# Four exponentials of a batch's token attention in one group instead of two pairs

## The reference

```
qkv = x @ W_qkv + b_qkv                      # per batch of 512 tokens
attn = (q @ k^T) * SCALE                     # 512 x 512
attn = attn * mult(sigmoid(attn))            # mult steps through 0.1, 0.3, 1, 1.5, 2
attn = softmax(attn)
out = (attn @ v) @ W_proj + b_proj
```

## Time and profile before

| | us |
|---|---|
| median of three runs | 492.12 |
| the profiled execution | 494.61 |
| its span, first to last instruction | 492.8 |
| PE busy | 476.9 |
| DVE busy | 315.8 |
| POOL busy | 310.8 |
| ACT busy | 263.2 |
| PE's granted clock, share of full | 0.996 |

### The profile page before, as it was taken

The page is one execution under the profiler, slowest core; times in us unless marked ns, Lnnn a source line. Parts: engine busy times, 40 slices in busy tenths (PEclk is TensorE's granted clock), DMA queues, the critical chain, the costliest instruction groups (busy, mean ns, idle before and its releaser), DMA issues.

```text
span 492.8 us, 6482 instructions
## 1 busy us (share of the span) xinstructions
PE 476.9 (97%) x2037; PEld 341.8 (69%) x2037; DVE 315.8 (64%) x724; ACT 263.2 (53%) x478; POOL 310.8 (63%) x314
## 2 busy tenths in 40 slices
PE   8898999998999998999999998999999999999997
PEld 7776766676676665676676766677666777778886
DVE  3747453655697758388855883569866565867563
ACT  3395636546725592338752659324773456355551
POOL 5364797429859383485563565467676585678773
PEclk9998999999999999999999999999999999999999
DMA  7700000000000000000000000000000000000000
GB/s 246 237 0 2 0 1 1 0 1 1 1 1 1 1 0 1 1 1 1 0 1 1 0 1 1 1 0 1 23 0 1 1 22 1 0 1 6 18 0 22
DMA packets 7934, 7.37 MB, mean 15 GB/s; under 512 B 732, under 2 KB 7772, under 8 KB 7900
## 3 DMA queue, kind: packets, MB, share of 16 engines
q1 hardware_dynamic: 7900, 6.96, 4.4%
HBM read 5.91 MB, written 1.05 MB: 14 GB/s over the span
## 4 chain that ended last, share of the span: by engine, by line
PE 78%; ACT 4%; DVE 3%; issue 2%; POOL 1%; DVEq 0%; ACTq 0%; POOLq 0%
PE bank L1308 19%; PE bank L1123 16%; PE bank L1125 16%; PE bank L1124 16%; PE bank L1346 3%; PE bank L1244 1%; PE bank L1146 1%; ACT L768 1%; DVE pr L1012 1%; PE bank L1338 1%; ACT xnB L665 1%; PE bank L1358 1%; PE bank L1316 1%; PE bank L1252 1%; PE bank L1286 1%
## 5 line engine op out<-in xcount | busy, mean ns | idle before, releaser
L645 POOL TENSOR_TENSOR t<-t,sl 128x512 f32<-128x512 f32 x105 | 147.7, 1413 | 84.5 <-DVE t L1064 65.2
L768 ACT ACTIVATE sl<-bank 128x512 f32<-128x512 f32 x168 | 99.2, 596 | 129.7 <-PE bank L1125 112.8
L1308 PE MATMUL bank<-t,WD 128*128 128x512 f32 x260 | 128.8, 592 | 0.0
L1064 DVE TENSOR_TENSOR t<-bank,sbc 128x512 f32<-128x512 f32 x105 | 72.3, 688 | 66.1 <-PE bank L1125 63.2
L1123 PE MATMUL bank<-xhF,WGh 128*128 128x512 f32 x167 | 90.6, 543 | 0.0
L645 POOL TENSOR_TENSOR t<-t,sbc 128x512 f32<-128x512 f32 x63 | 80.9, 1313 | 1.1 <-DVE t L1064 0.9
L1064 DVE TENSOR_TENSOR t<-bank,sl 128x512 f32<-128x512 f32 x63 | 43.2, 687 | 58.8 <-ACT sl L768 29.2
L1123 PE MATMUL bank<-xhF,WUh 128*128 128x512 f32 x168 | 67.0, 399 | 2.3 <-DVE t L1064 2.3
L1125 PE MATMUL bank<-xhF,WUl 128*128 128x512 f32 x168 | 66.7, 397 | 0.0
L1124 PE MATMUL bank<-xlF,WUh 128*128 128x512 f32 x168 | 66.5, 396 | 0.0
L1125 PE MATMUL bank<-xhF,WGl 128*128 128x512 f32 x167 | 66.4, 398 | 0.0
(11 more groups left out here) (209 smaller groups left out, 723.8 us busy)
## 6 DMA issues: line engine op xcount, KB each, us to landing
stage<-in_gate SPq DMA_DIRECT2D x7, 192.0 KB, 6.1
stage<-in_up SPq DMA_DIRECT2D x7, 192.0 KB, 6.3
WD<-in_down SPq DMA_DIRECT2D x7, 192.0 KB, 6.2
X<-in_x SPq DMA_DIRECT2D x4, 256.0 KB, 5.4
out<-X SPq DMA_DIRECT2D x3, 256.0 KB, 2.3
raw<-in_small SPq DMA_DIRECT2D x1, 384.0 KB, 4.3
out<-X SPq DMA_DIRECT2D x2, 128.0 KB, 2.1
raw<-in_small SPq DMA_DIRECT2D x1, 192.0 KB, 2.7
```

What stands on the lines that cost most here:

```text
L645: pool.tensor_tensor(t2[k % NT2][:, :], t2[k % NT2][:, :], by[:, :], ALU.mult).then_inc(a_done, 1)
L768: act.activation(sl[k % NSL][:, :], bank[k % 2][:, :], ACT.Silu).then_inc(silu_done, 1)
L1064: dve.tensor_tensor(t2[k % NT2][:, :], bank[2 + k % 2][:, :], by[:, :], ALU.mult).then_inc(t2_done, 1)
L1308: r = pe.matmul(OACC[:, :], WD[:, c, :], t2[k % NT2][:, :], start=(c == 0), stop=(c == CH - 1 or k == TAIL[0] - 1))
```

## The change

The two steps `bexp` 0 and `bexp` 1 are taken from offset 17 of each batch's thread and put at offset 23, ahead of `bexp` 2 and `bexp` 3. Nothing else is changed in the text.

```diff
--- before.py
+++ after.py
@@ -95,9 +95,9 @@
 ROUTED_LATE = (0, 1, 2)
 B_STEPS = [(0, "stats"), (1, "rstd"), (2, "xn"), (4, "xT"), (5, "xl"), (7, "bqk", 0), (8, "bqkl", 0), (11, "bs", 0), (11, "bsp", 0, 0), (12, "bsp", 0, 1), (12, "bsp", 0, 2), (13, "bsp", 0, 3),
            (14, "bs", 1), (14, "bsp", 1, 0), (15, "bsp", 1, 1), (15, "bsp", 1, 2), (16, "bsp", 1, 3),
-           (17, "bexp", 0), (17, "bexp", 1), (17, "bs", 2), (17, "bsp", 2, 0), (18, "bsp", 2, 1),
+           (17, "bs", 2), (17, "bsp", 2, 0), (18, "bsp", 2, 1),
            (18, "bsp", 2, 2), (19, "bsp", 2, 3), (20, "bs", 3), (20, "bsp", 3, 0),
-           (21, "bsp", 3, 1), (21, "bsp", 3, 2), (22, "bsp", 3, 3), (23, "bexp", 2), (23, "bexp", 3),
+           (21, "bsp", 3, 1), (21, "bsp", 3, 2), (22, "bsp", 3, 3), (23, "bexp", 0), (23, "bexp", 1), (23, "bexp", 2), (23, "bexp", 3),
            (25, "bpT", 0), (26, "bpT", 1), (26, "bpT", 2), (27, "bpT", 3),
            (28, "bo", 0), (29, "bo", 1), (30, "bw"), (30, "byx")]
 F_STEPS = [(0, "stats"), (1, "rstd"), (2, "xn"), (4, "xT"), (5, "xl"), (6, "route"), (7, "inner", 0), (8, "rt"), (9, "rexp"),
```

## The result

The changed kernel took 496.15 us (median of 20 runs, 494.09 to 498.05) against 493.37 us (20 runs, 490.76 to 495.64): ratio 1.0065, 95% interval [1.0047, 1.0083]. It is slower by 3.2 us, 2.3 to 4.1. The forecast was +1.37 us, within 1%: right in sign and in staying within 1%, but less than half of the size. Two single executions, 801.44 us of the kernel before and 965.86 us of a variant, were of a much slower state and are left out of every comparison.

What follows compares the result with a forecast made beforehand. PE, busy 97%, bounds the kernel, so ACT's relief counts only where PE waited. Terms -0.75 + 0 + 0 + 1.44 + 0.68 = +1.37 us on 492.12 give 493.5 us; range 489.3 to 497.1.

Steps and rivals of the forecast that it cites:

- Where the steps go: Planner's order: only ACT's queue changes; two exponentials per batch move from slots 49, 69, 86, 108 to 55, 75, 92, 114.
- Removed: Early block off ACT: eight table loads, 10.26 us; PE gains 0.75 us in batch 0, nothing in batches 1 to 3.
- Added, batch 0: Late Silu 56 ends 1.44 us later; PE stands 0.39 before gate 58, absorbed by L1012 behind POOL's run: 0 us.
- Rival A: Batch 0's early block was dearer, all three DVE waits go: -0.67 us, 491.5, or -2.79, 489.3; chance 0.17.
- rival B: POOL's bunched products lock DVE out in batches 1 to 3: +7.5 us, 499.6; chance 0.06.
- Batch 1: Late Silu becomes 249.46, gate product starts 249.95, 0.49 us to spare: 0 us, at most +0.95.
- Batch 2: Late block delays the copy PT by the full 1.44; PE's 1.39 wait becomes 2.83 less 0.57: +1.44 us.
- Batch 3: Late Silu ends at 366.37, gate product started at 365.69: +0.68 us, between 0 and 1.44.
- The base: Profiled execution 494.61 us, PE clock near full, so the +1.37 is carried over to the runs' median of 492.12.
- C: Every late block costs its full 1.44 us: +5.0 us, 497.1; chance 0.07.
- D: ACT's relief counts in full: -10.3 us, 481.9 (-2.1%); chance 0.03.
- E: The change does not do what it says, planner shifts other steps or loads stay: within +-1 us; chance 0.07.

Runs made afterwards that it cites:

- the last variant: Against the kernel before: batch 0's exponentials together, router's exponential ahead of batch 2's late pair and also of batch 0's four; 0.9989, 491.82 us.
- the kernel that beats both: Against the kernel before: batch 0's exponentials together, router's exponential ahead of batch 2's late pair, batches 1 and 3 unchanged; 0.9971 and 0.9932, 490.45 and 490.4 us.
- a third with the same wait 2 us later: The changed kernel with L1012 rewritten as four operations, against the kernel before; 1.0078, 496.71 us.

## Why the prediction was right or wrong, point by point

**Where the steps go: right.** PE's, DVE's and POOL's instructions stand in the same order in both kernels, and table loads fell by eight.

**Removed: right, and a little small.** The 0.75 us went, and PE went on behind it 0.98 us sooner; "it cannot be more" was wrong by 0.2 us, which the recorded idle time does not show. The 10.3 us less of ACT bought nothing else, as the windows of the earlier trace rows said. The changed kernel's trace again shows no drain beside a load: in batch 2 the last exponential ends at 297.15, the load starts at 297.26 and the Silu at 298.55.

**Added, batch 0: right for the trace in hand.** PE waits 0.19 and 0.25 us where 0.39 and 0.37 were worked out, and L1012 took the forecast 3.4 us. Batch 0 gave -1.01 us, not -0.75. But the trace shown was one of two outcomes of L1012. In the other the run times show a gain of 0.2 to 0.6 us; that nothing absorbs the late Silu there is argued. Rival A counted on an end of L1012's long wait, rival B on more such waits. It is the operation at which the run times part, but the change's trace neither ended its wait nor added another.

**Batch 1: 0, right. Batch 2: +1.44, measured +1.40. Batch 3: +0.68, measured +0.73,** with 0.47 recorded as idle.

**The sum: the step that failed is what I took to stand behind batch 2's wait, namely nothing.** "It moves the full 1.44" counted the wait and not what a longer wait does to PE. Behind it the granted clock was 0.50 for some 3.4 us, 1.62 us of loss, larger than any term of the sum. Shown: batch 2 alone gives 1.0057, all but batch 2 gives 0.9998, matmuls in the wait bring the clock back to 1.00 and 1.63 us with it, and where the fall happened to stay away (the changed kernel with L1012 rewritten) the same wait cost 1.41 us and nothing behind it. I had read PEclk only for the windows of the first pairs, and no term asked what PE does after the idle that the change lengthens.

**The base: "I carry the difference over" was the second omission.** The 493.5 us rest on a median of three runs, 492.12; twenty give 493.37, so 1.25 of the 2.65 us that the forecast time was short are the base's. And the profiled execution was in the upper of two groups. In the 20 runs of before some 11 were in it, in the 20 of after some 15; at 2.3 us or so between groups that is about +0.5 us. With -1.0 + 1.4 + 1.6 + 0.7 = +2.7 within the upper group it makes the measured +3.2. That putting batch 0 together raises the odds is not shown. For it: four variants with it had 10, 12, 11 and 10 of 12 runs in the upper group, and the last variant 12 of 12, against 16 of 35, 4 of 29 and 4 of 17 of the kernel before beside them. Against it: batch 2 alone, with batch 0 as before, had 10 of 12 beside the 16 of 35, and with batch 0 but not the rest together it was 5 of 12, 5 of 11 and 3 of 7, the last beside 9 of 16. So the cause of the odds stays open, and the 0.5 us is a count of runs, not a mechanism.

**Rivals.** A (batch 0's later waits go with the early block) did not occur: the 1.28 us before batch 0's transposes stayed. B (slower by over 1% through DVE held back in batches 1 to 3) did not occur: no PE wait for DVE there. C's size, +5.0, was not reached. D (ACT's relief counts in full) was rightly given little, and E did not occur: the order and the eight loads are as worked out.

## What to carry to other kernels

Fewer table loads help only where the engine that bounds the kernel waits for them; lengthening a block of the same engine somewhere else can cost more than the loads are worth, and here did. When a change lengthens a wait of PE, price the wait and, as a bound, a half-clock stretch behind it as a second term (1.6 us here). Put a small exponential beside the large ones it can share a load with, without delaying the large ones: that gave the kernel that beats both. And look at how the times of several runs are grouped before taking one profiled execution as the base of a sum.

## What the runs showed of the hardware

PE's granted clock can halve behind waits of about 2.2 us in a stream that is otherwise dense (0.50 for some 3.4 us, 1.6 us lost). It did so in the traces of two kernels and not in that of a third with the same wait 2 us later. All 20 runs of the changed kernel had a half-clock stretch somewhere, nine of 12 with batch 2 alone together, two of six of the third; no fall followed the waits of 1.39 us in the traces. A small DVE operation on SBUF operands that falls into a run of POOL products waits for one product (1.19 us) in some executions and for the whole rest of the run (4.84 us) in others of the same kernel. Written as four operations with one SBUF tensor and a scalar per partition each, every one of them waited for one product (1.18 to 1.31 us, 4.83 us for the four).
